# Attention on one core: softmax sums from spare value columns, small reciprocals through memory, a new order of the work

## The reference

```python
h = x + attention(layernorm(x)) @ Wo + bo     # x: (32, 164, 192), 12 heads of 16, window |i - j| <= 64
p = softmax(scale * q @ k.T + window_mask)    # per head, 164 x 164
attention = p @ v
```

## Time and profile before

| | before |
|---|---|
| median of 3 runs | 2708.12 us (2700.08 to 2710.7) |
| the profiled execution | 2715.21 us, its span 2713.5 us |
| TensorE busy over the span | 2499.4 us (92%) |
| VectorE, ScalarE, GpSimd busy | 1886.8, 1361.0, 241.0 us (70%, 50%, 9%) |
| attention, first scores of a step to the last residual | 459.4 to 1104.7 us |
| mean granted TensorE clock | 0.952 of full speed |

### The profile page before, as it was taken

How to read it: one execution, slowest core, us unless ns; L and a number is a source line. 1 busy time by engine, 2 the same in 40 slices (tenths; PEclk the granted TensorE clock), 3 DMA queues, 4 the chain that set the end, 5 groups by cost and what they waited for, 6 DMA issues and landing times.

```text
span 2713.5 us, 52437 instructions
## 1 busy us (share of the span) xinstructions
PE 2499.4 (92%) x21833; PEld 2305.7 (85%) x21833; DVE 1886.8 (70%) x2187; ACT 1361.0 (50%) x1314; POOL 241.0 (9%) x147
## 2 busy tenths in 40 slices
PE   8959984898898888299999999999999999999999
PEld 6736684777777777299999999999999999999999
DVE  7849924666667765387667676757877777777774
ACT  2238801232333332453535444357877777777770
POOL 2202201000000000111212121200000000000000
PEclk9989996888989997599999999999999999999999
DMA  3436513000000000000000000012000000000000
GB/s 112 131 84 153 146 36 147 9 16 11 17 17 13 14 17 10 16 15 18 27 24 17 24 17 24 14 54 99 24 24 20 20 24 23 20 20 27 20 16 9
DMA packets 84042, 103.78 MB, mean 38 GB/s; under 512 B 9063, under 2 KB 75127, under 8 KB 83191
## 3 DMA queue, kind: packets, MB, share of 16 engines
q1 hardware_dynamic: 80311, 91.48, 11.2%
q0 software_dynamic: 3616, 10.54, 1.5%
HBM read 71.63 MB, written 30.36 MB: 38 GB/s over the span
## 4 chain that ended last, share of the span: by engine, by line
PE 57%; DVE 1%; issue 0%; DMA 0%; POOL 0%; ACT 0%; SPq 0%; POOLq 0%; DVEq 0%
PE spline_acc L1660 31%; PE spline_acc L1643 9%; PE spline_acc L1642 8%; PE spline_acc L1644 8%; PE spline_xT L1623 0%; DMA spline_x<-h_scr 0%; DVE spline_weights_low L1367 0%; DVE spline_xn L569 0%; DVE spline_f L1400 0%; DVE spline_b L1383 0%; DVE spline_t L1388 0%; DVE spline_b L1377 0%; DVE spline_a L1372 0%; POOL spline_rstd L1339 0%; ACT spline_a L1531 0%
## 5 line engine op out<-in xcount | busy, mean ns | idle before, releaser
L1660 PE MATMUL spline_acc<-spline_weights,spline_f 128*128 128x192 f32 x5248 | 853.0, 326 | 0.0
L1660 PEld LDWEIGHTS spline_acc<-spline_weights,spline_f 128*128 128x128 f32 x5248 | 852.8, 190 | 0.0
L1408 DVE SCALAR_TENSOR_TENSOR spline_f<-spline_n,spline_b 128x2048 f32<-128x2048 f32 x164 | 375.7, 2291 | 183.9 <-PE spline_acc L1660 182.1
L1642 PE MATMUL spline_acc<-spline_f,spline_weights_high 128*128 128x328 f32 x1536 | 479.9, 312 | 7.2 <-DVE spline_f L1400 7.2
L1643 PE MATMUL spline_acc<-spline_f,spline_weights_high 128*128 128x328 f32 x1536 | 482.5, 314 | 0.0
L1644 PE MATMUL spline_acc<-spline_f,spline_weights_low 128*128 128x328 f32 x1536 | 476.4, 310 | 0.0
L1642 PEld LDWEIGHTS spline_acc<-spline_f,spline_weights_high 128*128 128x128 f32 x1536 | 290.0, 189 | 7.4 <-issue 7.4
L1400 DVE SCALAR_TENSOR_TENSOR spline_f<-spline_n,spline_a 128x984 fp32r<-128x984 f32 x128 | 151.0, 1180 | 200.0 <-PE spline_acc L1644 198.3
L1643 PEld LDWEIGHTS spline_acc<-spline_f,spline_weights_high 128*128 128x128 f32 x1536 | 289.2, 188 | 0.0
L1644 PEld LDWEIGHTS spline_acc<-spline_f,spline_weights_low 128*128 128x128 f32 x1536 | 288.8, 188 | 0.0
L942 ACT ACTIVATE attend_probs<-scores_by_key 82x1968 f32<-82x1968 f32 x64 | 115.7, 1809 | 287.6 <-PE scores_by_key L1077 287.6
(11 more groups left out here) (189 smaller groups left out, 3665.8 us busy)
## 6 DMA issues: line engine op xcount, KB each, us to landing
sample_pos<-pos_scr SPq DMA_DIRECT2D x32, 540.0 KB, 4.4
hid_scr<-spline_hid SPq DMA_DIRECT2D x64, 164.0 KB, 1.8
spline_xn<-hid_scr SPq DMA_DIRECT2D x41, 256.0 KB, 3.1
pix_scr<-stem_by_pixel SPq DMA_DIRECT2D x32, 225.0 KB, 2.5
sample_h<-pix_scr POOLq DMA_DIRECT2D x32, 225.0 KB, 4.4
spline_weights_raw<-w SPq DMA_DIRECT2D x1, 6144.0 KB, 23.6
spline_weights<-w SPq DMA_DIRECT2D x4, 1536.0 KB, 6.1
h_scr<-attend_h SPq DMA_DIRECT2D x16, 246.0 KB
```

The lines of the kernel that those rows point to most:

```text
L1408: nc.vector.scalar_tensor_tensor(f2[i][:], n_[u][:], MAGIC + i, b_[u][:], ALU.is_equal, ALU.mult).then_inc(f_ready, 1)
L1642: nc.tensor.matmul(z, high, x_high, start=start, stop=False)
L1660: last = nc.tensor.matmul(z, f2[i][:, r * P:(r + 1) * P], w2[:, i, r, :], start=(i == 0 and r == 0), stop=(i == 3 and r == 4 * CH - 1))
```

## The change

Sums: the values' tile `va` has 32 columns for each head and uses 16. The other 16 are now set to 1 once, so the product with the values also gives the sums, at partitions 32j + 16 to 32j + 31, and the 24 matmuls with the tile of ones are gone. `mix` is split by its two halves c of the keys; at i = 1 the first half moves up to q = 2.

Reciprocals: ScalarE copies the whole product to SBUF (`mix_out`, in place of `sums`). SyncE writes the four rows of sums to memory (4x492), reads them back as 48x41, VectorE takes one reciprocal of 48x41, and SyncE writes it to memory and reads it back four times, each spread over 32 partitions. The reciprocal stands one step later and `weigh` and `project_out` two steps later than the product they belong to.

The rest: `project_out` stands at q = 0 instead of q = 1. The values are copied by ScalarE instead of VectorE. The output's bias is a row of `wo` (the sums times their reciprocals are 1), so GpSimd's addition goes, and the residual's tokens are loaded once more, by SyncE. Both loads of tokens are issued between the two reciprocals of a pair. The window's mask is float32r instead of bfloat16, with one or two columns more in each piece.

The core of the diff:

```diff
-        X, Q, K_, V = (0, 1), (3, 4, 5), (8, 9, 10), (13, 16)
-        Y, SUM, MAX, MIX = (2, 12), (6, 14), (7, 15), (11, 17)
+        X, Q, K_, V = (0, 1), (3, 4, 5), (8, 9, 10), (12, 14)
+        Y, MAX, MIX = (2, 11), (7, 15), (6, 13)
...
+            def invert(t, i):
+
+                sp.wait_ge(mix_ready, 2 * t + i + 1)
+                sp.dma_start(total_scr[i], mixed[i][DH:P:32, :]).then_inc(total_out[i], 16)
+                sp.wait_ge(total_out[i], 16 * t + 16)
+                sp.dma_start(total[i][0:SUMS, :], total_scr[i].rearrange("j (k n) -> (j k) n", n=PART)
+                             ).then_inc(total_in[i], 16)
+                sp.wait_ge(inverted, 2 * t + i + 1)
+                sp.dma_start(rec_scr[i].rearrange("j (k n) -> (j k) n", n=PART), rec[i][0:SUMS, :]
+                             ).then_inc(rec_out[i], 16)
+                sp.wait_ge(rec_out[i], 16 * t + 16)
+                for j in range(4):
+                    sp.dma_start(spread[i][32 * j:32 * j + 32, :],
+                                 rec_scr[i, j:j + 1, :].rearrange("a n -> (a n)").partition_broadcast(32)
+                                 ).then_inc(spread_in[i], 16)
...
+            def between(t, u, first=False, more=True, more2=True):
+
+                if not first:
+                    leave(t - 1, 1 - u)
+                if more:
+                    load(sp, resid[1 - u], resid_in[1 - u], t + 1)
+                if more2:
+                    sp.wait_ge(xn_ready, t + 3)
+                    load(sp, x[u], x_in[u], t + 4)
...
+            with sp.Fori(1, PAIRS // 2 - 2) as tt:
                 for u in range(2):
-                    sp.wait_ge(resid_ready, 2 * tt + u + 1)
-                    sp.wait_ge(xn_ready, 2 * tt + u + 1)
-                    load(2 * tt + u + 2, u)
-                    leave(2 * tt + u, u)
-            for u in range(2):
-                leave(PAIRS - 2 + u, u)
+                    invert(2 * tt + u, 0)
+                    between(2 * tt + u, u)
+                    invert(2 * tt + u, 1)
+            for t in range(PAIRS - 4, PAIRS):
+                invert(t, 0)
+                between(t, t % 2, more=t < PAIRS - 1, more2=False)
+                invert(t, 1)
+            leave(PAIRS - 1, 1)
...
+            def invert(t, i):
+
+                dve.wait_ge(total_in[i], 16 * t + 16)
+                nc.vector.reciprocal(rec[i][0:SUMS, :], total[i][0:SUMS, :]).then_inc(inverted, 1)
+
+            def weigh(t, i):
+
+                dve.wait_ge(spread_in[i], 64 * t + 64)
+                nc.vector.tensor_tensor(oT[i][:].rearrange("p g n -> p (g n)"), mixed[i][:], spread[i][:],
+                                        ALU.mult).then_inc(weighed, 1)
...
+                    before = (t, 0) if i == 1 else None if first else (t - 1, 1)
+                    if not first:
+                        weigh(t - 1, i)
                     for q in range(4):
                         if i == 0 or more:
                             maximum(nxt, q)
...
+                        if q == 1 and i == 1 and more2:
+                            norm_out(tt + 1, u, use(t, X[1]))
+                        if q == 1 and before:
+                            invert(*before)
```

More of the change, by code:

```diff
@@ L896, in _ @@
                 low_k(0, g, start(START["K"][g]), HG + g + 1)
-            for i in range(2):
-                values(0, i, start(START["V"][i]))
             for q in range(4):
@@ L943, in expo, with pair @@
                                      ACT.Exp, scale=SCALE).then_inc(exped, 1)
-            def pair(tt, u, more=True):
+            def pair(tt, u, first=False, more=True):
                 t = 2 * tt + u
@@ L971, in _ @@
                 high(k1[0][:, g, :], start(START["K"][g]))
+            act.wait_ge(zeros_set, 5)
+            for i in range(2):
+                values(0, i, start(START["V"][i]))
             high(mh[:], start(START["MAX"]))
-            for u in range(2):
-                pair(0, u)
+            pair(0, 0, first=True)
+            pair(0, 1)
             with act.Fori(1, PAIRS // 2 - 1) as tt:
@@ L1134, in pair @@
-                        if q == 2 and more:
+                        if q == 0:
+                            if i == 0 and more:
+                                for j in range(2):
+                                    turn_x(t + 1, j, use(t, X[j]))
+                            if not first:
+                                project_out(a - 2, i, use(t, Y[i]))
+                        if q == 2:
                             if i == 0:
-                                read(use(t, X[0]), use(t, X[1]))
-                                for g in range(2):
-                                    project(wqh, wql, g, use(t, Q[g]))
-                            else:
-                                values(0, use(t, V[0]))
@@ L1141, in pair @@
-                    if i == 0 and more:
-                        project(wqh, wql, 2, use(t, Q[2]))
-                    pe.wait_ge(exped, 2 * a + 2)
-                    mix(u, i, use(t, SUM[i]), True)
+                                if more:
+                                    read(use(t, X[0]), use(t, X[1]))
+                                    for g in range(2):
+                                        project(wqh, wql, g, use(t, Q[g]))
+                            else:
+                                if more:
+                                    values(0, use(t, V[0]))
+                                mix(a, u, i, 0, use(t, MIX[i]))
@@ new lines, in pair @@
+                    if i == 0:
+                        if more:
+                            project(wqh, wql, 2, use(t, Q[2]))
+                        read(*(start(START["V"][j]) if first else use(t - 1, V[j]) for j in range(2)))
+                        for c in range(2):
+                            mix(a, u, i, c, use(t, MIX[i]))
+                    else:
+                        mix(a, u, i, 1, use(t, MIX[i]))
+                        if more:
+                            values(1, use(t, V[1]))
@@ L1145, in pair @@
                     if nxt:
                         turn_max(a + 1, use(t, MAX[i]))
-                    if more:
-                        if i == 0:
-                            for g in range(HG):
-                                project(wkh, wkl, g, use(t, K_[g]))
-                        else:
-                            values(1, use(t, V[1]))
-                    if i == 0:
-                        read(*(start(START["V"][j]) if first else use(t - 1, V[j]) for j in range(2)))
-                    mix(u, i, use(t, MIX[i]), False)
+                    if i == 0 and more:
+                        for g in range(HG):
+                            project(wkh, wkl, g, use(t, K_[g]))
```

259 lines of the change are left out of this document (124 added, 135 removed).

## The result

| | change | before, beside it |
|---|---|---|
| median of 4 runs | 2843.44 us (2834.58 to 2847.88) | 2709.41 us (2700.08 to 2713.55) |
| ratio to before, 95% interval | 1.0506 [1.0479, 1.0532] | |
| span of the profiled execution | 2846.2 us | 2713.5 us |
| first exponential to last residual | 776.0 us | 642.4 us |

A forecast was written before the change was run, and what follows sets the result against it. TensorE bounds attention now; the change adds waits for a chain through memory. Pairs 650.4 us, with low clock 710.4, plus start 36 and end 24.5: 771 against 645.3, +126, so 2834 us (range 2745 to 2905).

The forecast's parts named there:

- The chain: Through SyncE's DMAs, from pair t's reciprocal at i = 0 to that at i = 1: 24.5 us, 16.7 of it data.
- The pair that nobody stalls: A pair of attention steps without waits for memory: 37.3 - 3.8 + 1.1 = 34.6 us.
- The return: From the reciprocal of (t, 1) to that of (t + 1, 0): 20.3 us, plus 4 us for low clock.
- The wait: VectorE stops about 10 us before the reciprocal of i = 1, and TensorE behind it, needing the maxima.
- Rival A: Nobody waits in attention, as small transfers pass large ones or the data take few microseconds: 2675 us; chance 0.15.
- B: Half the wait, as loads overlap better or the store runs during the spreads: 5 us less a pair, 2760 us; chance 0.13.
- C: Low clock throughout: each stop of TensorE costs 8 us instead of 4, 2894 us; chance 0.15.
- (a): VectorE idles some 10 us before each of 15 reciprocals 48x41, until the totals' DMA; reciprocals of i = 0 without it.
- (b): The group of matmuls with ones is gone, and VectorE's reciprocal 48x41 takes near 405 ns.
- (c): In ScalarE's exponentials, pairs take 45 to 50 us, and are shorter from t = 12 on.
- (d): The DMA share is 0.14 for some 17 us a pair.
- (e): TensorE's clock is 0.50 right behind each stop, and less than 0.89 over the attention stage.

The follow-up runs named there:

- experiments 2 to 4: On the changed kernel: SyncE's transfers reordered 2695.39 us, transfers cut 2686.62, both 2682.48; a third group of loads 2895.46; loads issued by GpSimd 2734.78, by ScalarE 2806.75.
- experiment 3: The changed kernel with a third group of three loads, into a tile nobody reads, in 12 of 16 pairs: 2895.46 us, ratio 1.0694.
- experiment 5: Its exchange: output projection put ahead of the transposes, against the version with another order, cut transfers and bfloat16 mask (2675.12 us): 2683.81 us, ratio 0.9910.

## Why the prediction was right, and where its parts were off

**The chain: right.** From the reciprocal of (t, 0) to that of (t, 1) 24.5 us were forecast; for t = 1 to 11 it took 23.6 to 25.6, mean 24.3. Its parts, from the rows at 893.91: to the store's issue 4.0 (2.0 + 1.4 forecast), from there to the totals landed 18.4 (0.9 + 16.7 + 1.0 = 18.6), totals in 1.7 (2.0). For t = 0, without a store, the totals were back after 17.6 us, as forecast (landed at 510.71, and 1.7 for the way in), but the reciprocal stands at 20.0, since VectorE came to it later than they did; it is the same for t = 12 (20.7). For t = 13 and 14, where it waited, it was 20.0 and 19.0 where 19.6 was forecast. That small transfers do not pass large ones in one queue is shown by experiments 2 to 4 together: place in the queue decides, and a further group in front costs its 4.9 us. The rate that the prediction sets aside, 2.0 us plus the bytes over 436 GB/s, is given by the Trainium skill ("DMA: Bandwidth & Descriptors", anatomy of one DMA) for transfers that GpSimd issues, and these are SyncE's; the sum did not use it.

**The pair that nobody stalls: right.** 34.8 us at full clock in the version with another order, 34.6 forecast. Its two parts swap a microsecond: 13.3 us up to the reciprocal of i = 1 (14.3 forecast) and 21.5 back (20.3). The moved projection, taken as 0 with bounds of 0.9, costs 1.0.

**The return: somewhat too short.** From (t, 1) to (t + 1, 0) it took 26.2 us as a mean of t = 1 to 11, where 20.3 + 4 was forecast. At full clock it is 21.5 (the version with another order; there TensorE is at 1.00 in the 5 us behind each of these reciprocals of i = 1, where the change has 0.50 to 0.73), so the clock's part is 4.7. The pair was 50.5 us and not 48.8, and with the start (36.5; 36) and the end (23.5; 24.5) attention comes to 779 us instead of 771.

**The wait: wrong in size, "about 10 us" per reciprocal.** There were 14 waits with a mean of 5.9, and 6.1 for t = 1 to 11. The step that failed is that TensorE would come to the wait at full speed. It did so three times, and there the wait is 10.2 to 10.9 us. As a mean of the eleven it comes 24.3 - 6.1 = 18.2 us after the last reciprocal, where 14.3 was forecast and 13.3 is what it takes at full clock, for it spends much of this stretch at 1.2 GHz, as at 893 to 903. Windows from a reciprocal of i = 0 on, the first before a wait of 10.23 us, the second before one of 4.02:

```profile
945.64:959.00 13.36, 11.59 (x247) 9.75 (x245) 7.75 (x12) 4.60 (x9) 0.00 (x0) 1.00 0.21 54
...
893.91:913.90 19.99, 18.74 (x254) 15.25 (x254) 7.64 (x12) 4.55 (x9) 0.00 (x0) 0.63 0.18 50
```

The first does the same work in 13.4 us at full clock for which the second needs 20.0. The sum did not notice: the chain's end is set by the DMAs, and a slow TensorE only shortens the wait in front of it. Two windows from reciprocal to reciprocal of the changed kernel:

```profile
840.06:893.91 53.85, 45.15 (x544) 37.24 (x543) 20.80 (x45) 13.74 (x19) 1.00 (x1) 0.60 0.09 26
...
945.64:997.00 51.36, 37.43 (x553) 31.62 (x551) 20.82 (x45) 13.52 (x19) 1.01 (x1) 0.77 0.10 27
```

Against 34.84 and 29.32 busy at full clock, the mean of the eleven pairs is 50.5 with TensorE busy for 41.4: 12.1 of the 15.6 us more are slower matmuls and 3.6 are idle time. Read from busy times, the clock would be to blame for three quarters; read along the chain, for 4.7 us. The runs decide for the chain: with the wait's cause removed most of the low clock went too (from 468 us of attention to 183 in the version with another order, summed as in experiment 3), and one more group of loads cost 4.9 us a chain.

**Rival A** (nobody waits, 2675 us) named the price well: removing the blockade gave 2682 to 2695, and 2675 with the mask. Of its two conditions, that small transfers pass large ones did not occur; that the data between the chains take few microseconds is what the cut transfers brought about (7 us; it had put the limit at 8.3). **B** (2760) and **C** (2894) did not come; C's 8 us of clock per stop lies beyond the 4.7.

**Not foreseen:** the spreads as the next late link. Without the wait at the reciprocal they cost 50.1 us, so rival A, priced with only that wait gone, would have missed 46 us (2720.66 against 2675).

**The signs named ahead:** (a) the wait is there, of 5.9 us and not 10, in 14 of the reciprocals of i = 1 (not at t = 0 and 12) and in none of i = 0; (b) 406 ns for 405, the ones gone; (c) from exponential to exponential 47 to 55 us in the third to the twelfth pair, then 47.8, 37.5 and 45.9; (d) a share of 0.24 to 0.13 for 18 us; (e) 0.59 and 0.50 behind the stop in the rows of the result, mean 0.70; that it would be low ahead of most stops too was not foreseen.

## What to carry to other kernels

In these runs a small transfer on which an engine waits was as late as the large ones in front of it in its queue. Before a chain through memory is put beside existing transfers, measure from the trace what those take when they are alone (issue to the end of the data, not their bytes over a peak rate), and put them behind the chain's links or cut them so that more engines share them; here each was worth some 150 us (148 and 157), and both together hardly more (161). Another engine's queue only moves the cost, where that engine has work of its own. And price a wait along the chain that sets it; busy time and clock of the waiting engine tell how the time is filled, not why it passes.

## What the runs showed of the hardware

Transfers of 82 and 46 partitions moved at 39 to 44 GB/s and a share of two of 16 DMA engines; cut into 80 + 2 and 32 + 14, with the same bytes, they moved at 130 GB/s and a share of 0.52, and left 6.7 of 82.9 us of the totals' wait. The Trainium skill's rule on the number of engines ("DMA: Bandwidth & Descriptors", on why a semaphore counts to 16: the largest number up to 16 that divides the slowest dimension) agrees: 80 and 32 divide by 16, 82 only by 2.

Issuing is not free behind busy transfers: SyncE took 2.98 us for a load that it issues in 0.33 us in the version with another order, and ScalarE up to 4.56, in which it computes nothing.

Removing TensorE's short waits did not bring its clock back in proportion: the exchange of experiment 5 has 70 us of them at TensorE, against 78 in the version without it, and its low-clock time in attention was 220 us against 176. A saving in a stage whose clock moves between the two levels is not a saving until it is timed.
